# A GpSimd subtraction that waits for VectorE, and one of two small transposes moved along TensorE's queue, in a two-layer attention kernel

## The reference, cut to what matters

```python
q, k, v = to_heads(x @ w_in.T)                       # self; cross: x @ Wq, ctx @ Wk, ctx @ Wv, with biases
scores = einsum('bhqd,bhkd->bhqk', q, k) * scale     # self: plus ALiBi bias, -inf above the diagonal
attn = softmax(scores)                               # subtracts the largest score of each row
x = layernorm(x + (attn @ v) @ w_out)
```

## Time and profile before

| | |
|---|---|
| median of three runs | 1715.83 us |
| profiled execution, its own time | 1715.96 us |
| its span, first to last instruction | 1714.2 us |
| attention | from the start to about 950 us |
| TensorE matmul busy | 1455.4 us, 85% |
| VectorE busy | 1073.8 us, 63% |
| ScalarE busy | 975.7 us, 57% |
| GpSimd busy | 630.5 us, 37% |
| mean granted TensorE clock | 0.924 of full speed |

### The profile page before, as it was taken

How to read it: one execution, slowest core, us unless ns; L and a number is a source line. 1 busy time by engine, 2 the same in 40 slices (tenths; PEclk the granted TensorE clock), 3 DMA queues, 4 the chain that set the end, 5 groups by cost and what they waited for, 6 DMA issues and landing times. The chain is left out here.

```text
span 1714.2 us, 43611 instructions
## 1 busy us (share of the span) xinstructions
PE 1455.4 (85%) x17896; PEld 1208.5 (71%) x17896; DVE 1073.8 (63%) x2277; ACT 975.7 (57%) x1419; POOL 630.5 (37%) x615
## 2 busy tenths in 40 slices
PE   5999999999999999999998672234999999999950
PEld 3777777777777777777776332134999999999940
DVE  3667777676777777777776357793545454445425
ACT  3667676767676767677776110023654565546507
POOL 1644444444443232322220000075354455445326
PEclk9999999999999999999999795556999999999975
DMA  5011111111112222222211530005334343432239
GB/s 180 21 58 57 58 57 57 57 58 57 48 49 75 76 86 72 82 76 76 76 52 39 161 87 6 0 0 158 79 54 91 92 98 52 97 93 45 29 59 356
DMA packets 129795, 129.54 MB, mean 76 GB/s; under 512 B 28288, under 2 KB 116464, under 8 KB 129600
## 3 DMA queue, kind: packets, MB, share of 16 engines
q1 hardware_dynamic: 114496, 106.29, 20.2%
q0 software_dynamic: 15104, 20.48, 7.4%
HBM read 82.54 MB, written 44.20 MB: 74 GB/s over the span
## 5 line engine op out<-in xcount | busy, mean ns | idle before, releaser
L495 ACT ACTIVATE at_pr<-at_A 128x2048 f32<-128x2048 f32 x128 | 240.7, 1881 | 152.6 <-PE at_A L325 152.6
L589 DVE TENSOR_REDUCE at_mx<-at_A 128x12 f32<-128x1536 f32 x128 | 224.6, 1755 | 37.7 <-PE at_A L292 33.7
L34 PE MATMUL ex_D<-ex_w,ex_hT 128*128 128x256 f32 (+1 forms) x1920 | 233.8, 282 | 0.4
L34 PEld LDWEIGHTS ex_D<-ex_w,ex_hT 128*128 128x128 f32 (+1 forms) x1920 | 230.4, 184 | 3.1 <-DVE ex_raw L1429 1.9
L34 PE MATMUL ex_U<-ex_xT,ex_w 128*128 128x384 f32 (+1 forms) x1152 | 221.7, 351 | 0.0
L719 POOL TENSOR_SCALAR_AFFINE_SELECT at_pr<-at_pr 128x2048 f32<-128x2048 f32 x64 | 128.5, 2007 | 241.2 <-ACT at_pr L495 241.2
L1485 POOL DMA_INDIRECT total<-ex_o,ex_ids x80 | 131.6, 1645 | 229.3 <-DVE ex_o L1434 197.7
L34 PEld LDWEIGHTS ex_U<-ex_xT,ex_w 128*128 128x128 f32 x1152 | 206.9, 189 | 7.3
L1419 DVE TENSOR_TENSOR ex_hT<-ex_h,ex_hT 128x384 fp32r<-128x384 f32 (+1 forms) x192 | 112.7, 587 | 96.5 <-ACT ex_hT L1379 96.5
L325 PE MATMUL at_A<-at_qp,at_kt 32*128 32x256 f32 x2048 | 140.7, 390 | 0.0
L341 PE MATMUL at_C<-at_pr,at_v 128*32 128x128 f32 x4096 | 138.4, 276 | 1.0 <-ACT at_oq L502 1.0
(11 more groups left out here) (189 smaller groups left out, 2763.6 us busy)
## 6 DMA issues: line engine op xcount, KB each, us to landing
ex_w_in<-in_w SPq DMA_DIRECT2D x16, 1024.0 KB, 6.8
at_turned<-in_x_turned SPq DMA_DIRECT2D x16, 512.0 KB, 4.6
at_x<-in_x SPq DMA_DIRECT2D x16, 512.0 KB, 4.0
x<-at_y SPq DMA_DIRECT2D x32, 256.0 KB, 2.4
at_x<-x SPq DMA_DIRECT2D x16, 512.0 KB, 3.9
at_turned<-in_ctx_turned SPq DMA_DIRECT2D x16, 512.0 KB, 4.7
rows<-at_y SPq DMA_DIRECT2D x32, 256.0 KB, 2.2
total<-at_y SPq DMA_DIRECT2D x32, 256.0 KB, 2.9
```

What stands on the lines that cost most here:

```text
L34: last = nc.tensor.matmul(out, pick_l(left, a), pick_r(right, b), start=(start and n == 0), stop=(stop and n == 2))
L495: nc.scalar.activation(pr[:, k % 2].rearrange("p i n a q -> p (i n a q)"), A[:].rearrange("p i n a q -> p (i n a q)"), ACT.Exp).then_inc(e ...
L589: nc.vector.tensor_reduce(mx[:, k % 2, 0:12], A[:, 0:3].rearrange("p i n a k -> p (i n a) k"), AX, ALU.max).then_inc(max_done, 1)
```

## The change

On TensorE, `turn_max` of an odd set is taken out of the head of its own iteration and put into the even iteration before it, directly behind `weigh`. It writes to the bank `C[1]` instead of `C[0]`, so that it waits for `t_done` (the normalising that reads `C[1]`) instead of `o_copied`. `weigh(k)` now names its wait for `copy_o(k-1)` itself, and `set_back` of an odd set waits until `take_max` has read `C[1]`. On VectorE `take_max` of an odd set goes into the even iteration too, and `residual` is cut in two so that it stands between the addition and the statistics (now `deviation`). On GpSimd `source_lo(g + 2)` gets a wait for `m2_ready >= k + 3`, which is raised by the split (L599) of the maxima of set `k + 2`.

```diff
             def turn_max(k):
                 pe.wait_ge(m2_ready, k + 1)
-                if k >= 2:
+                if k % 2 == 0 and k >= 2:
                     pe.wait_ge(o_copied, k - 1)
-                b = C[0][:, :].bitcast(BF16)
+                elif k >= 3:
+                    pe.wait_ge(t_done, k - 2)
+                b = C[k % 2][:, :].bitcast(BF16)
...
                 pe.wait_ge(v_done, 2 * g + np_ + 1)
-                pe.wait_ge(mt_done, min(k + 2, sets))
-                if k == sets - 1:
-                    pe.wait_ge(o_copied, k)
+                pe.wait_ge(mt_done, min(k + 2 - (k + 1) % 2, sets))
+                wait(pe, o_copied, k)
                 b = C[0]
...
                 if k >= 1:
                     pe.wait_ge(t_done, k)
+                pe.wait_ge(mt_done, min(k + 2 + k % 2, sets))
                 b = C[1]
...
-                turn_max(k)
+                if k % 2 == 0:
+                    turn_max(k)
                 if k + 1 < sets:
                     maxima(k + 1)
...
                 if k >= 1:
                     weigh(k - 1)
+                if k % 2 == 0:
+                    turn_max(k + 1)
                 if k % 2 == 1 and k >= 3:
                     output_back((k - 3) // 2)
...
                 nc.vector.tensor_copy(mT[:, k % 2].rearrange("p n q -> p (n q)"),
-                                      C[0][:, :].bitcast(BF16)[:, 0:2 * P]).then_inc(mt_done, 1)
+                                      C[k % 2][:, :].bitcast(BF16)[:, 0:2 * P]).then_inc(mt_done, 1)
...
                                         ALU.add).then_inc(res_done, 1)
+
+            def deviation(u):
                 dve.wait_ge(res_done, u + 1)
...
-                take_max(k)
+                if k % 2 == 0:
+                    take_max(k)
                 if k + 1 < sets:
                     reduce_max(k + 1)
...
-                if s == 0 and g >= 1:
-                    residual(2 * g - 2)
-                if s == 2 and g >= 1:
-                    residual(2 * g - 1)
+                if s % 2 == 0 and g >= 1:
+                    residual(2 * g - 2 + s // 2)
+                if k % 2 == 0:
+                    take_max(k + 1)
+                if s % 2 == 0 and g >= 1:
+                    deviation(2 * g - 2 + s // 2)
...
                 if s == 2 and g + 2 < groups:
+                    pool.wait_ge(m2_ready, k + 3)
                     source_lo(g + 2)
```

More of the change, by code:

```diff
@@ L699, in _ @@
             residual(halves_of - 2)
+            deviation(halves_of - 2)
             normalise_set(sets - 1)
@@ L702, in _ @@
             residual(halves_of - 1)
+            deviation(halves_of - 1)
         @block.gpsimd
```

## The result

| | before | after |
|---|---|---|
| median | 1715.86 us | 1688.62 us |
| ratio of after to before | | 0.9844, 95% interval 0.9826 to 0.9862 |
| span of the profiled execution | 1714.2 us | 1686.4 us |
| end of attention | 956.6 us | 929.4 us |
| self-attention group (groups 3 to 13) | 29.20 us | 27.74 us |

The kernel became 27.2 us faster by the medians, where 24.3 were forecast. In the two profiled executions the span fell by 27.8 us, and all but 0.6 us of that lies in attention, whose end moved by 27.2 us. A group is measured as in the earlier trace rows, from one exponential of set 0 to the next.

The account below looks back on a forecast made before the run. TensorE in attention was taken as bound by stalls behind a VectorE cast that GpSimd's subtraction holds. 1715.96 - 15.9 (GpSimd's wait) - 8.4 (moved transposes) = 1691.7, predicted as 1691.5 us; range 1686 to 1708.

Parts of the forecast that it names:

- The bound and its cause: Attention: `output_back` stalls 14 times, 14.9 us in all, for normalising queued behind a VectorE cast held by GpSimd's subtraction.
- Part 1: GpSimd's subtraction waits for the split, removing 13 stalls of 1.12 us and one of 1.3: 15.9 us.
- Part 2: Odd set's transposes moved behind `weigh`: 0.12 us in each of 62 even iterations, 1.0 in the last group, 8.4 together.
- the term x: Even iteration, time from the moved `turn_max` to the projection: taken at 0.13 us, bounds 0.13 and 0.39.
- The other two terms: Even iteration after the change: `weigh` to `turn_max` 1.01 us, projection to `maxima` 1.50 + 0.09.
- The last group: No projection there; `turn_max` of sets 125 and 127 loses its wait for the copy: 1.0 us counted for both.
- The waits of the moved transposes: Extra waits in TensorE's queue, behind `weigh` on `m2_ready` and `t_done`: long satisfied, cost nothing.
- A: Rival, chance 0.15: GpSimd's wait pays, moving the transposes does not; about 1700 us.
- B: Rival, chance 0.10: moving the transposes costs 0.14 us in 62 iterations, `turn_max` to projection at its upper end; about 1708 us.
- C: Rival, chance 0.07: GpSimd's subtraction, now just ahead of the normalising, holds it on VectorE; slower, about 1748 us.
- D: Rival, chance 0.03: GpSimd's wait does not remove the collision, only the moved transposes' gain is left; about 1707 us.
- the signs named for right: Casts and splits 0.18 us, no `output_back` wait, self-attention groups 27.8 us, cross-attention 0.24 shorter, `weigh` to `maxima` 2.73.

Follow-up runs that it names:

- part 2 alone: The changed kernel without GpSimd's wait for the split ahead of the subtraction: 1709.65 us, ratio 0.9961 to the kernel before.
- the wait on the wrong semaphore: The changed kernel with GpSimd's wait on the reduction (`max_done`) instead of the split (`m2_ready`): 1721.83 us, ratio 1.0033 to the kernel before.

## Why the prediction was right, point by point

**The bound and its cause.** Right. With the cast free, `output_back` waits for nothing, and cutting the subtraction in four without moving it gives the same gain. The rule of the Trainium skill (SBUF — State Buffer, Who interferes with whom) on the shared port agrees in all its parts that a run here shows: the hold ends with the GpSimd instruction (cast to 519.44, subtraction to 519.41), L599 with its two SBUF inputs is held in the four-piece kernel, and in the changed kernel the normalising (its L625), with one, runs beside L722 at its usual 0.42 us.

**Part 1, 15.9 us.** Right: 15.1 (12.4 to 18.0) alone, with groups of 28.07 us as forecast from group 1. That nothing late came up behind GpSimd's wait was right as well.

**Part 2, 8.4 us.** The mechanism is right, the size was too small: 0.17 us an even iteration and not 0.12. The step is the term x. It was taken at 0.13, which was also called its lower bound, and measured 0.07. The time of the two weight loads was not a lower bound, since the projection's first load starts before the second of them has ended (201.31, 201.38, with loads of 0.11 us for the pair). The other two terms, 1.01 and 1.59, came out at 1.02 and 1.59. (The 0.22 in the working of the 1.59 is 0.23 in the earlier trace rows, which changes little.) The last group gave 0.87 us up to its last exponential, where 1.0 was forecast. The rule on weight loads (the Trainium skill, TensorE: Matmul & The Clock Gate, Part 3, The mechanism), by which x would have been near 0.4, is not borne out: the projection's load went in 0.07 us behind the transposes' on the same rows.

**The waits of the moved transposes.** The prediction held them to be long satisfied. In group 1 one is not. There GpSimd splits the cross-attention's weights, and L604 of set 7 is held for 1.12 us by one of those instructions, as L599 was before:

```profile
74.57 1.12 DVE L604 TENSOR_TENSOR at_m<-at_mx,at_m 128x16 bf16<-128x16 f32 x1
75.11 0.81 PEld L342 LDWEIGHTS at_C<-at_pr,at_v 128*32 128x32 f32 x32 [0.33 <-issue]
75.89 0.42 DVE L625 TENSOR_TENSOR at_on<-at_C,at_rden 128x256 f32<-128x256 f32 x1
76.43 0.13 PEld L305 LDWEIGHTS at_C<-at_ident_b,at_m 128*128 128x128 bf16 x2 [0.51 <-issue]
```

The normalising ends at 76.31, and the transposes, which now need it, start 1.32 us behind `weigh` instead of 1.01. Before, the same hold cost nothing (6.89 us for this interval, as without a hold); now the interval is 7.04 us where the other groups have 6.72. That is why group 1 gained nothing (28.07 before, 28.06 after). The move takes one wait away and brings TensorE closer to another.

**What the sum missed.** By the two traces the 27.8 us of the span are made up so: 15.95 us in the intervals from set 3 to set 0 of groups 2 to 30 (forecast 15.9), 10.0 us in their 58 even iterations (forecast 7.4 in 62), 1.3 us in the last group to the end of attention (forecast 1.0). Three more pieces were in no term: 0.3 us less before the first exponential, 0.4 us more in groups 0 and 1, 0.6 us less behind attention. The first and the last lie where the change alters nothing, so the 0.5 us that the three give together is luck. The rest of what the change did better, 2.6 of about 3 us, is the 0.05 us by which each even iteration gained more, for the most part x. In the sum the two parts were added as if they did not touch. For the change as a whole this did no harm, because the holds were gone. The expectation for part 2 alone, 11.3 us, was too high by 4.6 us for this reason, since the move makes every hold longer. The cost of nothing that was given to `take_max` ahead of the statistics holds only with GpSimd's new wait: without it, the later statistics bring the collision into cross-attention.

**Group 0.** It took 27.66 us against 27.27. The difference is in its first interval, 6.90 us against 6.35, where the mean granted clock was 0.81 against 0.90 of full speed. The kernel before is the odd one there: the other nine traces have 0.79 to 0.83 and 6.85 to 7.12 us, also those of kernels in which nothing was moved. So this is the clock of one execution and not the change.

**The rivals.** A (the move does not pay) fell with 27.70 us in cross-attention. B (x near 0.4) fell with 0.07. C (L722 holds the normalising) fell with 0.42 us beside the subtraction. D (the collision stays) did not come; part 2 alone shows that it would have given 1709.65 us and not the 1707 worked out for it, and with the wait on the wrong semaphore it is 1721.83. Of the signs named for right, all came but for sizes: self-attention groups are at 27.74 us and not 27.8, cross-attention groups fell by 0.35 us and not 0.24, both because of x, and one cast, of set 62 at 457.07, took 0.32 us instead of 0.18 beside another GpSimd instruction, at no cost.

## What to carry to other kernels

A small VectorE instruction that reads and writes SBUF, ahead of something that TensorE waits for, should be kept apart from long GpSimd instructions: let GpSimd wait until just behind it, or cut GpSimd's work into pieces shorter than the slack. Measure that slack as hold minus stall, for each place in the queue by itself; what lies under it is free. And when an edit shifts one engine against another, look at which overlaps it lengthens: here the second edit alone gave back about two fifths of its expected gain through the very collision that the first one removes. When a buffer is swapped to get rid of a wait, ask who writes the new one next, and what the moved instruction now waits for instead.

## What was not expected of the hardware

VectorE gets in between GpSimd instructions that follow each other without a wait: in the four-piece kernel two of its instructions were held once each, for 0.17 and 0.47 us, and not until the last piece had ended. Cutting the subtraction cost GpSimd 2.79 us instead of 2.37. Two bf16 transposes behind `weigh` cost 0.07 us, and a second pair behind them 0.11.
